# The guard against non-finite values in the front chunks moves from VectorE to GpSimd and ScalarE

## The reference

```python
def bitnet_linear(x, weight, scale_param):
    s = jnp.maximum(jnp.mean(jnp.abs(weight), axis=1), 1e-08)
    binary_w = jnp.sign(weight / s[:, None])
    y = jnp.einsum('bsi,oi->bso', x, binary_w)
    y = y * (s * scale_param)[None, None, :]
    return jnp.nan_to_num(y, nan=0.0, posinf=1000000.0, neginf=-1000000.0)
...
x = x + 0.5 * ffn(layernorm(x))     # base W (512 x 512) + bias, plus 2 of 8 LoRA experts of rank 16
x = x + attn(layernorm(x))          # q, k, v, o through bitnet_linear; 32 heads of 16, 8 kv heads
x = x + 0.5 * ffn(layernorm(x))
```

## Time and profile before

| | us |
|---|---|
| median of 3 runs | 1210.61 (1208.24 to 1212.01) |
| the profiled execution's own time | 1210.39 |
| its span | 1208.6 |
| busy PE, DVE, ACT, POOL | 1081.1, 876.0, 708.4, 306.2 |
| six front chunks alone | 0 to 238 |
| bodies 0 and 1, bodies 2 to 6, body 7 | about 118 each, 112.2 each, about 87 |
| tail | the last 60 |

### The profile page before, as it was taken

One profiled execution on the slowest core, in us unless ns is written; L12 is line 12 of the kernel. 1 busy time (PEld: TensorE's weight loads), 2 busy tenths in 40 slices (PEclk: granted clock), 3 DMA queues, 4 the chain that ended last, 5 costly groups with the idle time before them and its releaser, 6 DMA issues.

```text
span 1208.6 us, 19276 instructions
## 1 busy us (share of the span) xinstructions
PE 1081.1 (89%) x5944; PEld 491.6 (41%) x5944; DVE 876.0 (72%) x1259; ACT 708.4 (59%) x1313; POOL 306.2 (25%) x527
## 2 busy tenths in 40 slices
PE   1877676699999999999999999999999999999857
PEld 1666564334433342334333433443343334333336
DVE  3676869677787778787778777868886787782164
ACT  2343432365776667676667666756765676668511
POOL 4134345610241033141032104210510241032010
PEclk9997989699999999999999999999999999999968
DMA  7012133121121111300300021103101200200300
GB/s 244 18 53 83 53 92 103 33 69 36 32 55 32 38 30 46 77 25 25 77 24 24 24 79 31 34 26 77 27 24 47 54 24 24 77 6 6 87 0 36
DMA packets 87331, 59.03 MB, mean 49 GB/s; under 512 B 44144, under 2 KB 73328, under 8 KB 87280
## 3 DMA queue, kind: packets, MB, share of 16 engines
q1 hardware_dynamic: 87280, 58.39, 16.7%
HBM read 37.64 MB, written 20.32 MB: 48 GB/s over the span
## 4 chain that ended last, share of the span: by engine, by line
PE 73%; DVE 16%; ACT 5%; issue 3%; POOL 1%; DMA 1%; SPq 0%; DVEq 0%; ACTq 0%; POOLq 0%
PE ps_out L1226 19%; PE ps_score L1214 18%; PE ps_max L1193 15%; PE ps_fill L1151 6%; DVE neg_max L1015 3%; PE ps_fill L1178 2%; DVE neg_max L1073 2%; ACT probs L786 2%; PE ps_fill L1124 2%; PE ps_out L1151 2%; PE ps_fill L1155 1%; DVE xt_l L968 1%; DVE zd L927 1%; PE ps_fill L1136 1%; PE ps_max L1207 1%
## 5 line engine op out<-in xcount | busy, mean ns | idle before, releaser
L786 ACT ACTIVATE probs<-ps_score 128x512 f32<-128x512 f32 x1024 | 555.8, 595 | 275.1 <-PE ps_score L1214 273.5
L1015 DVE TENSOR_REDUCE neg_max<-ps_max 128x1 f32<-128x1024 f32 x480 | 571.4, 1218 | 175.7 <-PE ps_max L1193 174.6
L1214 PE MATMUL ps_score<-qst,kst 99*128 99x512 bf16 x1024 | 319.8, 386 | 11.0 <-ACT probs L786 7.8
L1193 PE MATMUL ps_max<-kst,qst 96*128 96x512 bf16 x1024 | 290.0, 384 | 20.7 <-DVE neg_max L1073 12.4
L1226 PE MATMUL ps_out<-probs,v_ring 128*32 128x512 f32 x2048 | 274.5, 608 | 0.0
L1214 PEld LDWEIGHTS ps_score<-qst,kst 99*128 99x128 bf16 x1024 | 88.1, 97 | 287.6 <-ACT probs L786 243.5
L1193 PEld LDWEIGHTS ps_max<-kst,qst 96*128 96x128 bf16 x1024 | 89.2, 98 | 137.5 <-DVE neg_max L1073 21.8
L307 POOL TENSOR_TENSOR wait_pad<-wait_pad 1x1 bf16<-1x1 bf16 x75 | 16.3, 217 | 395.9 <-DVE neg_max L1015 335.0
L1226 PEld LDWEIGHTS ps_out<-probs,v_ring 128*32 128x32 f32 x2048 | 40.4, 108 | 90.7 <-issue 90.3
L1124 PE MATMUL ps_fill<-ident,xn 128*128 128x128 f32 x192 | 32.1, 292 | 37.1 <-ACT xn L735 25.7
L735 ACT ACTIVATE xn<-xc,ln_shift,rstd 128x512 f32<-128x512 f32 x48 | 38.1, 810 | 41.0 <-POOL ln_shift L574 40.5
(11 more groups left out here) (202 smaller groups left out, 1276.5 us busy)
## 6 DMA issues: line engine op xcount, KB each, us to landing
qst<-q_dram SPq DMA_DIRECT2D x192, 64.0 KB, 2.2
q_dram<-zm SPq DMA_DIRECT2D x24, 256.0 KB, 2.6
kst<-k_dram SPq DMA_DIRECT2D x192, 32.0 KB, 2.1
xc<-x SPq DMA_DIRECT2D x8, 512.0 KB, 3.9
x_dram<-xc SPq DMA_DIRECT2D x8, 512.0 KB, 2.9
xc<-x_dram SPq DMA_DIRECT2D x8, 512.0 KB, 4.1
out<-xc SPq DMA_DIRECT2D x8, 512.0 KB, 2.8
att_dram<-att SPq DMA_DIRECT2D x31, 128.0 KB, 2.0
```

The lines of the kernel that those rows point to most:

```text
L786: act.activation(probs[:, kt % 2, j, :], ps_score[j % 2][:, :], ACT.Exp, scale=1.0 / HD ** 0.5).then_inc(probs_ready, 1)
L1015: dve.tensor_reduce(neg_max[:, uu % 2, t:t + 1], ps_max[max_slot(uu, pos)][:, :, :], AXY, ALU.max, negate=True).then_inc(max_read, 1)
L1193: last = pe.matmul(ps_max[slot][:, half, :], qst[0:SR, r, j, q * P:(q + 1) * P], kst[0:SR, r, half * 512:half * 512 + 512], start=True, st ...
L1214: pe.matmul(ps_score[j % 2][:, :], kst[0:SR + PARTS, uu, kt * P:(kt + 1) * P], qst[0:SR + PARTS, uu, j, :], start=True, stop=True).then_in ...
```

## The change

- **Guard of all front chunks.** ScalarE writes the scaled projections to zd (not z), and at C it writes their negative to z. GpSimd does both clamps as minimum with 0, then maximum with -1e6: of zd into zneg, and of the negative into its own place (zpos is z). The sum becomes zneg minus zpos, again in z. The mask is zd * 0 + 0 into zneg, written by GpSimd at once behind: it is zero where the value is finite and NaN elsewhere, so P copies the clamped value into zd only where the value is not finite. No mask and no clamp of a front chunk is left on VectorE.
- **Short pieces.** GpSimd's subtractions at S1 and S3 are done in pieces of 512, 512 and 256 columns.
- **Four score banks** in units 30 and 31: scores 2 and 3 of a step go to the ps_max buffer that the turn doesn't use.
- **Casts of the feed-forward weights** on ScalarE stand behind T1b of chunk 0, their remainders on VectorE behind T1bl of chunk 0, ahead of chunk 1's statistics.

The rest of the diff splits the counters of the guard into several semaphores. Its core:

```diff
-FRONT_ON_DVE = ("clamp", "sum")
+FRONT_ON_DVE = ()
...
+        def four_score_banks(i, uu):
+            return isinstance(i, int) and UB * i + uu >= NU - 2
+        def score_bank(i, uu, j):
+            if four_score_banks(i, uu) and j >= 2:
+                return ps_max[1 - turn_slot(uu, True)][:, j - 2, :]
+            return ps_score[j % 2][:, :]
...
+                if ch.front:
+                    gp.wait_ge(negated[s], ch.n * 3 + piece + 1)
+                    gp.tensor_scalar(zneg[s][:, cols], zd[s][:, cols], 0.0, -BIG, ALU.min, ALU.max).then_inc(clamped[s], 1)
+                    gp.tensor_scalar(zpos[s][:, cols], z[s][:, cols], 0.0, -BIG, ALU.min, ALU.max).then_inc(clamped[s], 1)
+                    return
...
+                if ch.front:
+                    gp.tensor_tensor(zpos[s][:, cols], zneg[s][:, cols], zpos[s][:, cols], ALU.subtract).then_inc(clamp_sum[s], 1)
+                    return
...
-                gp.tensor_scalar(zneg[s][:, cols], z[s][:, cols], 0.0, 0.0, ALU.mult, ALU.add).then_inc(guard_step[s], 1)
+                value = zd[s] if ch.front else z[s]
+                gp.tensor_scalar(zneg[s][:, cols], value[:, cols], 0.0, 0.0, ALU.mult, ALU.add).then_inc(mask_ready[s], 1)
...
+                    for a0 in range(0, KQ, 512):
+                        piece = slice(a0, min(a0 + 512, KQ))
+                        rest = kq[:, piece] if k == 1 else parts[s][:, 2, piece]
+                        last = gp.tensor_tensor(rest, kq[:, piece], parts[s][:, k - 1, piece], ALU.subtract)
+                    last.then_inc(part_rest[s], 1)
...
+                if pos in ("C0", "C1", "C2") and ch.front:
...
+                    act.wait_ge(filler_read[bnk], reads + 1)
+                    act.activation(z[s][:, cols], zd[s][:, cols], ACT.Copy, scale=-1.0).then_inc(negated[s], 1)
...
             for k, item in enumerate(ALONE):
                 fill(item)
+                if item[0].n == 0 and item[1] == "T1b" and item[0].slot == 0:
+                    ffn_weights()
...
-                if step[0] == "G" and ch.front:
-                    dve.wait_ge(clamp_sum[s], ch.sum0 + (k + 1))
-                    dve.tensor_scalar(mask, z[s][:, cols].bitcast(I32), INF_BITS, INF_BITS, ALU.bitwise_and,
-                                      ALU.bitwise_xor).then_inc(guard_step[s], 1)
...
+                if four_score_banks(i, uu) and kt == 0 and j >= 2:
+                    pe.wait_ge(max_read, max_use(i, 1, 16) + 1 if uu == 2 else turn_use(i, 2, True) + 1)
+                elif four_score_banks(i, uu) and kt > 0:
+                    pe.wait_ge(probs_ready, i * (32 * UB) + (32 * uu + 4 * kt + j - 3))
```

More of the change, by code:

```diff
@@ L217, in macaron @@
         z = [t[:, 0:ZW] for t in zm]
+        zpos = z
         zneg = [t[:, ZW:2 * ZW] for t in zm]
@@ L280, in macaron @@
         guard_step = [sem(f"guard_step{s}") for s in range(2)]
+        negated = [sem(f"negated{s}") for s in range(2)]
+        mask_ready = [sem(f"mask_ready{s}") for s in range(2)]
         part_cast = [sem(f"part_cast{s}") for s in range(2)]
@@ L635, in fill @@
                     clamped_sum(ch, k)
[L636 to L639, removed]
+                    not_finite(ch, k)
                 if pos in ("S1", "S3") and not ch.on_dve("split"):
@@ L711, in _, with ffn_weights @@
         def _(act):
-            act.wait_ge(ffn_in, 5 * 16)
-            act.activation(wr_hl[:, :, 0:E], wr_raw[:, :, :], ACT.Copy).then_inc(ffn_hi, 1)
-            for dst, src in ((a_h, raw_a), (wb_h, raw_wb), (b_h, raw_b)):
-                act.activation(dst[:], src, ACT.Copy).then_inc(ffn_hi, 1)
+            def ffn_weights():
+                act.wait_ge(ffn_in, 5 * 16)
+                act.activation(wr_hl[:, :, 0:E], wr_raw[:, :, :], ACT.Copy).then_inc(ffn_hi, 1)
+                for dst, src in ((a_h, raw_a), (wb_h, raw_wb), (b_h, raw_b)):
+                    act.activation(dst[:], src, ACT.Copy).then_inc(ffn_hi, 1)
             def attn_weights():
@@ L766, in fill @@
                         a0 = 512 + (m0 + m) * CH
-                        last = act.activation(z[s][:, a0:a0 + CH], ps[:, m * CH:(m + 1) * CH], ACT.Copy,
+                        last = act.activation(zd[s][:, a0:a0 + CH], ps[:, m * CH:(m + 1) * CH], ACT.Copy,
                                               scale=col_scale[:, 2 + m0 + m:3 + m0 + m])
                     last.then_inc(filler_read[bnk], 1)
+                if pos in ("C0", "C1", "C2") and ch.front:
+                    k = int(pos[1])
+                    cols = slice(512 * k, 512 * k + 512)
+                    bnk, reads = ch.bank(("VK", "Q0", "Q1")[k])
+                    act.wait_ge(filler_read[bnk], reads + 1)
+                    act.activation(z[s][:, cols], zd[s][:, cols], ACT.Copy, scale=-1.0).then_inc(negated[s], 1)
                 if pos == "VT":
@@ L918, in guard @@
                     dve.tensor_scalar(zneg[s][:, cols], z[s][:, cols], 0.0, 0.0, ALU.mult,
-                                      ALU.add).then_inc(guard_step[s], 1)
-                if step[0] == "G" and ch.front:
-                    dve.wait_ge(clamp_sum[s], ch.sum0 + (k + 1))
-                    dve.tensor_scalar(mask, z[s][:, cols].bitcast(I32), INF_BITS, INF_BITS, ALU.bitwise_and,
-                                      ALU.bitwise_xor).then_inc(guard_step[s], 1)
+                                      ALU.add).then_inc(mask_ready[s], 1)
                 if step[0] == "P":
-                    dve_wait(dve, guard_step[s], ch.guard0 + (2 * k + 1))
+                    dve_wait(dve, mask_ready[s], ch.sum0 + (k + 1))
                     if ch.front:
-                        dve.copy_predicated(zd[s][:, cols], mask, z[s][:, cols]).then_inc(guard_step[s], 1)
+                        dve.copy_predicated(zd[s][:, cols], mask, zpos[s][:, cols]).then_inc(guard_step[s], 1)
                     else:
@@ L985, in fill @@
                     dve.wait_ge(x1_loaded[s], 16)
-                    dve.wait_ge(guard_step[s], ch.guard0 + 4)
+                    dve.wait_ge(guard_step[s], ch.sum0 + 2)
                     for t in range(CT):
@@ L1075, in _ @@
                 fill(item)
-                if item[0].n == 0 and item[0].slot == 1 and item[1] == "LN1c":
+                if item[0].n == 0 and item[0].slot == 0 and item[1] == "T1bl":
                     ffn_weights()
@@ L1171, in fill @@
                 if pos == "VT":
-                    pe.wait_ge(guard_step[s], ch.guard0 + 2)
+                    pe.wait_ge(guard_step[s], ch.sum0 + 1)
                     for u in range(CT):
@@ L1211, in score @@
             def score(i, uu, kt, j):
-                if not isinstance(i, int) or 32 * (UB * i + uu) + 4 * kt + j >= 2:
+                if four_score_banks(i, uu) and kt == 0 and j >= 2:
+                    pe.wait_ge(max_read, max_use(i, 1, 16) + 1 if uu == 2 else turn_use(i, 2, True) + 1)
+                elif four_score_banks(i, uu) and kt > 0:
+                    pe.wait_ge(probs_ready, i * (32 * UB) + (32 * uu + 4 * kt + j - 3))
+                elif not isinstance(i, int) or 32 * (UB * i + uu) + 4 * kt + j >= 2:
                     pe.wait_ge(probs_ready, i * (32 * UB) + (32 * uu + 4 * kt + j - 1))
-                pe.matmul(ps_score[j % 2][:, :], kst[0:SR + PARTS, uu, kt * P:(kt + 1) * P],
+                pe.matmul(score_bank(i, uu, j), kst[0:SR + PARTS, uu, kt * P:(kt + 1) * P],
                           qst[0:SR + PARTS, uu, j, :], start=True, stop=True).then_inc(scores_ready, 1)
```

17 lines of the change are left out of this document (6 added, 11 removed).

## The result

The changed kernel takes **1223.56 us** (median of 8 runs, 1217.23 to 1226.07) beside 1210.94 us (8 runs, 1208.24 to 1212.99). The ratio is 1.0096, its 95% interval 1.0072 to 1.0120: slower by 0.7 to 1.2%. The forecast was 1215.7 in a range of 1202 to 1224. The direction was right, the size was less than half of what was measured.

The account below looks back on a forecast made before the run. In the front stage VectorE's guard work between pairs bounds the kernel, in the bodies TensorE. - 5.8 + 16.6 - 1.6 - 1.2 - 2.7 = + 5.3 us on 1210.39 gives 1215.7 us, range 1202 to 1224.

Parts of the forecast that it names:

- GpSimd's queue: Between two pairs: pieces, norms, waits, bias pair and splits sum to 33.85 us, plus 2.4 for meetings with predicated copies.
- the two transitions: Stretches between front pairs: GpSimd's longer queue delays WR, + 8.3 us each, + 16.6 together; bounds + 5.2 and + 12 each.
- Start, - 5.8: First front chunks: casts moved behind chunk 0's transposes let chunk 1's norm start at 23.6 in place of 29.39 us.
- the third rival: Front chunks: the first clamp stays at 1.93 us, + 15.6 us more over both stretches, 1231 us; chance 0.08.
- Behind the last mask: End of each stretch on VectorE: predicated copy 0.65, expert weights 1.3, one bias meeting up to 1.25 us, then WR.
- Third pair, - 1.6: Third front pair: masks leave VectorE's chain of maxima, 1.7 us, shorter meetings give 0.4, split pieces take 0.6; - 3 to 0.
- Bodies 0 and 1, - 1.2: First two bodies: three masks fewer on VectorE, three copies more on ScalarE, - 0.6 us each; bounds - 2.5 to + 1.
- Units 30 and 31, - 2.7: Last units: four score banks shorten the step loop from 2.88 to 2.5 us, some seven times 0.4; - 4 to - 1.
- Short pieces: GpSimd's split in pieces: forecast as a cost only, 0.6 us at the end of the third pair.
- The first two rivals: Between pairs: blocking is free, 1209.5 us, chance 0.25; GpSimd instructions overlap, guard piece 2.4 us, 1203.7 us, chance 0.20.

Follow-up runs that it names:

- late_casts: The kernel before with only the feed-forward casts moved behind T1b of chunk 0, on ScalarE and VectorE; 1204.39 us, ratio 0.9948.
- max_first: The changed kernel with both GpSimd clamps of the front chunks written maximum first, minimum second; 1259.48 us, ratio 1.0395.
- bias_later: The changed kernel with GpSimd's slot 1 bias adds held back until VectorE has written w_rep of the next pair's slot 0; 1216.41 us, ratio 1.0048.
- no_guard: The changed kernel without its guard part, which stays on VectorE; late casts, short pieces and four banks kept; 1199.24 us, ratio 0.9901.
- short_pieces: The kernel before with only GpSimd's subtractions S1 and S3 cut into 512, 512 and 256 columns; 1208.46 us, ratio 0.9977.
- swap_no_guard: no_guard with GpSimd's first clamp (third pair and all bodies) written minimum first, maximum second; 1195.16 us, ratio 0.9864.
- pieces_256: no_guard with GpSimd's subtractions in five pieces of 256 columns in place of 512, 512 and 256; 1199.56 us, ratio 0.9906.
- four_banks: The kernel before with only the four score banks in units 30 and 31; 1207.02 us, ratio 0.9970.

## Why the prediction was right and where it was not

The sign and the mechanism were right: GpSimd's queue takes the place of VectorE's and is longer. The size was + 5.3 us, the trace shows + 13.1: 4.3 us of the difference arose in the two transitions and 3.8 in the third pair. That the time came to lie in the range was luck in part: 1223.56 is 0.4 us below its upper end and outside the forecast's own 1212 to 1222.

- **Start, - 5.8.** Right: - 5.7, and the norm of chunk 1 starts at 23.72 us, forecast 23.6 (timeline of GpSimd). late_casts alone gives 0.52%, the gain reaches the end.

```profile
23.72 0.23 POOL L580 TENSOR_SCALAR var_eps<-meanvar 128x2 f32<-128x2 f32 x1 [0.45 <-DVE meanvar L980]
```

- **GpSimd's queue.** Forecast 36.25 us from the first clamp to the last mask with the meetings, measured 35.86 (63.15 to 99.01). Both clamps take 0.61 us, as taken from the second clamp's row, and max_first shows that the order of the two operations sets this. So the third rival (one of the clamps stays slow) was false, and its price was right: I gave it 7.8 us a transition for one slow clamp, and max_first has 16.2 for two.
- **Behind the last mask: the step that was sized wrong.** I wrote 0.65 for the copy and 1.3 for the weights, with one meeting of up to 1.25. Measured: 1.78, 2.57 and 1.34 with the gaps, 5.87 us to the transpose of w_rep, 2.7 more than I had. I had GpSimd's losses in the meetings counted with care (0.5 each) and VectorE's hardly at all. bias_later shows it: without the bias adds the three steps take 1.94 us, and the period falls by 3.6. The transitions came out at + 10.0 and + 10.9, forecast + 8.3 each, bounds + 5.2 and + 12.
- **Third pair, - 1.6.** Wrong in sign: + 2.2. no_guard has + 2.0 and short_pieces + 1.5 there, so the guard need not be the cause. I gave the pieces 0.6 at the end. What I left out is TensorE's clock, as the interval shows, before and then in the changed kernel (columns as above):

```profile
160.56:275.23 114.67, 91.17 (x459) 48.90 (x460) 86.67 (x126) 43.98 (x80) 51.62 (x58) 0.88 0.24 71
175.81:292.68 116.88, 95.92 (x459) 52.91 (x460) 83.20 (x120) 47.64 (x86) 46.37 (x74) 0.83 0.23 70
```

  The same 459 matmuls keep TensorE busy for 4.8 us more at a mean clock of 0.83 in place of 0.88, while its idle time falls by 2.5. From 170 to 175 us, ahead of WR, TensorE did nothing and the clock stood at 0.50, it was still 0.50 from 175 to 180 and 0.55 from 180 to 185. So nine matmuls of the first feed-forward pass take 4.14 us behind the transition and 2.30 under full clock (chain of the changed kernel):

```profile
34.39 2.30 PE ps_fill L1176 x9
...
180.44 4.14 PE ps_fill L1176 x9
```

  The clock is not all of it: the same nine take 4.10 us in swap_no_guard, which is back at 114.56 by its faster clamp.
- **Bodies 0 and 1, - 1.2.** The size was near, - 1.9, by luck. I put it on the masks that leave VectorE, but max_first has the masks on GpSimd as well and gets nothing (118.98). It is not GpSimd's first clamp either, for pieces_256 still has the slow one and takes 117.43. The intervals from WR to WR of before, the changed kernel and pieces_256, a clamp of pieces_256 in it, and five microseconds of before:

```profile
275.23:394.23 119.00, 115.03 (x655) 45.41 (x654) 90.34 (x112) 81.39 (x153) 29.11 (x46) 0.99 0.14 38
292.68:409.82 117.14, 113.33 (x655) 45.20 (x654) 89.19 (x109) 82.88 (x156) 27.51 (x53) 1.00 0.14 39
268.65:386.08 117.43, 113.47 (x655) 45.16 (x655) 90.32 (x112) 81.35 (x153) 30.25 (x54) 1.00 0.14 39
316.58 1.93 POOL L601 TENSOR_SCALAR zd<-zm 128x512 f32<-128x512 f32 x1 [17.01 <-ACT zm L774]
370.00:375.00 5.00, 3.64 (x15) 1.07 (x16) 2.44 (x3) 1.57 (x3) 0.07 (x1) 0.66 0.00 0
```

  The difference is TensorE's busy time, and with it the clock: before, it falls to 1.2 GHz once in this interval, between 370 and 375 us (mean 0.66 there), in the changed kernel and in pieces_256 it doesn't. All kernels of the table with about 119.0 us have a mean of 0.99 in this interval and all with 117.1 to 117.4 have 1.00. In the 36 or 37 us around that point, TensorE's waits are the same in before, the changed kernel, pieces_256 and swap_no_guard (1.5, 1.0, 0.3 and 0.2 us), so what decides whether the clock falls stays open.
- **Units 30 and 31, - 2.7.** Right in sum: - 2.7 in the trace, and 0.30% for four_banks alone. The step was not: I forecast 2.5 us in place of 2.88. Scores of consecutive steps in the changed kernel come 2.6 to 2.9 us apart:

```profile
1124.70 0.60 PE L1243 MATMUL ps_score<-qst,kst 99*128 99x512 bf16 x2
...
1127.40 0.79 PE L1243 MATMUL ps_score<-qst,kst 99*128 99x512 bf16 x2
...
1130.27 0.61 PE L1243 MATMUL ps_score<-qst,kst 99*128 99x512 bf16 x2
...
1132.89 0.59 PE L1243 MATMUL ps_score<-qst,kst 99*128 99x512 bf16 x2
```

- **Short pieces.** I saw only their price, 0.6 us in the third pair. Alone they are 0.23% faster, by 1.2 and 3.6 us in the two transitions of short_pieces. So measured from no_guard (a period of 56.70 us) the guard costs 10.6 and 14.2 us in the two transitions. The forecast of + 8.3 didn't suffer from that, as it counted GpSimd's queue in the changed kernel to an instant and compared it with 160.56 of before; what the pieces win lies on VectorE's path, which that queue replaces.

The first two rivals, blocking for free and overlapping GpSimd instructions, are both refuted: by the row of 1.78 us, and by pieces of 3.45 us (63.15 to 66.60) where 2.95 was the point of decision.

## What to carry to other kernels

Work that was moved to GpSimd to relieve VectorE cost twice here: once in GpSimd's own queue, where it stood behind everything that was there, and once on VectorE, where clamps, casts, copies and router steps waited for the GpSimd instruction that was running. Price both sides of a meeting, VectorE's with up to the whole length of GpSimd's instruction, and look at what stands at the end of the queue ahead of the engine that waits. Where work must be on GpSimd, cut long instructions, keep others away from VectorE's last steps, and try both orders of a two-operation instruction before moving it anywhere. And where an interval changes by one or two microseconds, read the granted clock of it before naming a cause.

## What was not expected of the hardware

- The order of the two operations in one GpSimd clamp of 512 columns changes its time by a factor of three: minimum first 0.61 us, maximum first 1.92 us, for the same values (max_first, swap_no_guard).
- A VectorE instruction of 4 columns that takes 0.17 us alone took 2.19 us beside a GpSimd subtraction of 1280 columns and 0.72 beside pieces of 512; four of 8 columns took 2.66 in place of 0.85 us. In this kernel cutting the subtractions was worth 0.23%, and keeping the bias adds away from the router steps about 0.5%.
- The predicated copy is among the instructions that meet: 1.78 us beside a bias add, 0.73 without. The layer norm's statistics are not: 0.69 us beside a split.
- One fall of TensorE's clock to 1.2 GHz between the WR of body 0 and that of body 1 lengthened an interval of 117.2 us by some 1.8, in some kernels and not in others, with the same waits of TensorE around it.
